# One turn number per piece of work, and the first loads in the order of their first use, in a fused decoder kernel

## The reference

```
out_t = r_t . (u * k_t v_t + s);   s = k_t v_t + w_t * s        (w = exp(-exp(...)))
```

## Time and profile before

| | |
|---|---|
| three runs | 692.63, 693.77, 694.01 us |
| profiled execution | span 694.0 us; no other time is recorded for it |
| busy of the span | TensorE 93%, VectorE 86%, ScalarE 82%, GpSimd 45% |
| mean granted TensorE clock | 0.985 of full |
| moved by DMA | 50.4 MB |

### The profile page before, as it was taken

How to read it: one execution, slowest core, us unless ns; L and a number is a source line. 1 busy time by engine, 2 the same in 40 slices (tenths; PEclk the granted TensorE clock), 3 DMA queues, 4 the chain that set the end, 5 groups by cost and what they waited for, 6 DMA issues and landing times.

```text
span 694.0 us, 17297 instructions
## 1 busy us (share of the span) xinstructions
PE 645.3 (93%) x5877; PEld 561.6 (81%) x5877; DVE 598.2 (86%) x1430; ACT 571.7 (82%) x2071; POOL 311.6 (45%) x440
## 2 busy tenths in 40 slices
PE   6878998999999999999999999999999989898776
PEld 5666787888989888988989888989888877687555
DVE  3598588999999999999999999999999987968274
ACT  1568899899999999999999999999999987664513
POOL 1154252646464554636364646454554624432120
PEclk9999999999999999999999999999999999999799
DMA  8920031221305050504122231305050503120200
GB/s 306 325 70 9 2 104 36 70 70 58 88 9 138 1 146 1 145 2 122 25 85 62 67 81 53 93 4 144 1 146 1 146 0 108 31 70 0 69 9 8
DMA packets 53725, 50.44 MB, mean 73 GB/s; under 512 B 6030, under 2 KB 48902, under 8 KB 53254
## 3 DMA queue, kind: packets, MB, share of 16 engines
q1 hardware_dynamic: 53638, 49.34, 24.7%
HBM read 28.62 MB, written 3.93 MB: 47 GB/s over the span
## 4 chain that ended last, share of the span: by engine, by line
PE 80%; DVE 8%; ACT 7%; issue 3%; POOL 1%; DMA 0%; SPq 0%; DVEq 0%; ACTq 0%; POOLq 0%
PE PS_B L552 16%; PE PS_T L654 9%; PE PS_B L694 8%; PE PS_S L552 7%; PE PS_D L559 5%; PE PS_S L625 4%; PE PS_T L662 4%; PE PS_S L559 4%; PE PS_T L559 4%; ACT SC L1291 3%; PE PS_D L800 2%; PE PS_B L703 2%; PE PS_D L552 2%; ACT PT L1301 2%; PE PS_T L545 2%
## 5 line engine op out<-in xcount | busy, mean ns | idle before, releaser
L1291 ACT ACTIVATE SC<-SC,NMX 128x128 f32<-128x128 f32 x512 | 200.0, 398 | 0.2
L1291 ACT ACTIVATION_READ_ACCUMULATOR SC<-SC,NMX 128x1 f32 x512 | 101.0, 197 | 0.0
L654 PE MATMUL PS_T<-CST,SC 128*128 128x128 f32 x512 | 81.3, 281 | 7.7 <-ACT PT L1301 3.6
L976 DVE TENSOR_REDUCE NMX<-SC 128x4 f32<-128x512 f32 x128 | 85.2, 676 | 0.4 <-POOL SC L1499 0.3
L1301 ACT ACTIVATE PT<-PS_T 128x512 f32<-128x512 f32 x120 | 70.8, 590 | 12.7 <-PE PS_T L654 12.7
L654 PEld LDWEIGHTS PS_T<-CST,SC 128*128 128x128 f32 x512 | 56.4, 141 | 26.1 <-ACT PT L1301 12.7
L1057 DVE TENSOR_TENSOR_SCAN SS<-W,AJ 128x1024 f32<-128x1024 f32 x32 | 73.2, 2288 | 0.2
L552 PE MATMUL PS_B<-MX,W 128*128 128x128 f32 x512 | 64.2, 280 | 4.7 <-ACT KR L1350 4.7
L552 PEld LDWEIGHTS PS_B<-MX,W 128*128 128x128 f32 x512 | 61.3, 196 | 4.9 <-ACT KR L1350 4.9
L1499 POOL TENSOR_TENSOR SC<-SC,MADD 128x512 f32<-128x512 f32 x48 | 59.9, 1276 | 6.5 <-DVE SC L956 6.5
L552 PE MATMUL PS_B<-B_LT,W 128*128 128x128 f32 x512 | 61.1, 278 | 1.0 <-ACT B_LT L1231 0.9
(11 more groups left out here) (231 smaller groups left out, 1595.0 us busy)
## 6 DMA issues: line engine op xcount, KB each, us to landing
W<-EW SPq DMA_DIRECT2D x32, 512.0 KB, 4.1
V<-values_by_head SPq DMA_DIRECT2D x28, 512.0 KB, 5.4
W<-in_weights SPq DMA_DIRECT2D x1, 4160.0 KB, 21.0
ENC<-in_enc SPq DMA_DIRECT2D x16, 128.0 KB, 2.3
out<-X SPq DMA_DIRECT2D x16, 128.0 KB, 5.8
X<-in_x SPq DMA_DIRECT2D x1, 1920.0 KB, 15.7
values_by_head<-VC SPq DMA_DIRECT2D x14, 128.0 KB, 1.8
W<-in_weights SPq DMA_DIRECT2D x1, 1280.0 KB, 8.5
```

The lines of the kernel that those rows point to most:

```text
L654: last = pe.transpose(PS_T[:, j * T:(j + 1) * T], SC[:, nr(b, a) % 2, g, j, :], ident)
L976: dve.tensor_reduce(NMX[:, nr(b, a) % 2, GH * g:GH * g + GH], SC[:, nr(b, a) % 2, g], AX_X, ALU.max, negate=True)\
L1291: last = act.activation(SC[:, nr(b, a) % 2, g, j, :], SC[:, nr(b, a) % 2, g, j, :], ACT.Exp, bias=NMX[:, nr(b, a) % 2, h:h + 1], accum_out ...
```

## The change

Three edits. The pieces and their instances are the same before and after; nothing is computed otherwise.

1. Each entry of an order has a turn number instead of a lag, and a second table, `*_MOVED`, gives single sequences a number of their own. The engine's program is all instances sorted by 10000 b + number, so the order may differ from one sequence to the next. On TensorE 97 of 757 instances that do something leave the old order, on VectorE 273 of 1225, on ScalarE 276 of 897, on GpSimd 64 of 316, on SyncE 25 of 75.
2. The stores of sequences 2 to 11 stand together on SyncE, between `b_vspread@13` and `b_wspread@14`; stores 0 and 1 stand a few sequences later than before.
3. The loads: tokens of sequences 1 and 2 and `enc` of sequence 0 go ahead of the second block of weights, the cross masks of the first three sequences come right behind it, the rest of the tokens and masks behind the third block. A new semaphore `in_next` counts the first three sequences' loads; sequence 3 (`AHEAD`) waits for `in_rest`.

```
-                if 0 <= i - lag < B:
-                    pieces[name](i - lag, arg)
+            for name, arg, b in in_order(order, moved):
+                pieces[name](b, arg)
+def in_order(order, moved):
+    turns = [(TURN * b + moved.get((name, arg), {}).get(b, turn), name, arg, b)
+             for name, arg, turn in order for b in range(B)]
+    return [(name, arg, b) for _, name, arg, b in sorted(turns, key=lambda t: t[0])]
...
             sp.dma_start(MASK[:, B, :], mask_self).then_inc(in_rows, 16)
+            sp.dma_start(X[:, 1:AHEAD, :], x[1:AHEAD].rearrange("b s c -> s b c")).then_inc(in_next, 16)
+            sp.dma_start(ENC[:, :], enc[0]).then_inc(in_enc, 16)
             sp.dma_start(W[:, W_AT["ao"]:W_CUT1], weights[:, W_AT["ao"]:W_CUT1]).then_inc(in_wa, 16)
-            sp.dma_start(ENC[:, :], enc[0]).then_inc(in_enc, 16)
-            sp.dma_start(MASK[:, 0:B, :], mask_cross.rearrange("b q k -> q b k")).then_inc(in_rest, 16)
-            sp.dma_start(X[:, 1:B, :], x[1:B].rearrange("b s c -> s b c")).then_inc(in_rest, 16)
+            sp.dma_start(MASK[:, 0:AHEAD, :], mask_cross[0:AHEAD].rearrange("b q k -> q b k")).then_inc(in_next, 16)
             sp.dma_start(W[:, W_CUT1:W_CUT2], weights[:, W_CUT1:W_CUT2]).then_inc(in_wb, 16)
+            sp.dma_start(X[:, AHEAD:B, :], x[AHEAD:B].rearrange("b s c -> s b c")).then_inc(in_rest, 16)
+            sp.dma_start(MASK[:, AHEAD:B, :], mask_cross[AHEAD:B].rearrange("b q k -> q b k")).then_inc(in_rest, 16)
...
                 elif b == 1:
+                    dve.wait_ge(in_next, IN_REST)
+                elif b == AHEAD:
                     dve.wait_ge(in_rest, IN_REST)
```

More of the change, by code:

```diff
@@ L70 @@
 LAST = 2
+AHEAD = 3
 FIRST = 4
@@ L84 @@
     ('d_keyrec', 0, 15): 4, ('d_val', 0, 15): 2}
+TURN = 10000
 SP_ORDER = [
-    ("b_vspread", 0, 4), ("d_store", 0, 6), ("b_wspread", 0, 3), ("b_vstore", 0, 3), ("a_load", 0, 0)]
-PE_ORDER = [
[L90 to L99, removed]
@@ L100 @@
-DVE_ORDER = [
[L101 to L118, removed]
@@ L133 @@
-POOL_ORDER = [
[L134 to L140, removed]
+    ("a_load", 0, 90000), ("b_wspread", 0, 110006), ("b_vstore", 0, 120002), ("b_vspread", 0, 120004),
@@ new lines @@
+POOL_MOVED = {
+    ("a_root", 0): {0: -50000, 1: -59992, 2: 5517, 3: -623, 6: 487}, ("a_addmask", (0, 0)): {0: -49996, 2: 7940},
+    ("a_addbias", 0): {0: -49990, 1: -59988, 4: 9187, 5: 9655, 6: 9538},
+    ("a_addmask", (0, 2)): {0: -49994, 1: 15130, 2: 8105, 5: 9860, 10: 13909},
+    ("a_root", 1): {1: 18156, 2: 22639, 4: 19843, 9: 22805, 10: 22624, 12: 21685},
+    ("a_addbias", 1): {3: 21198, 4: 19848, 5: 20647, 7: 25047}, ("a_addmask", (1, 0)): {0: 26178, 1: 22179},
+    ("a_addmask", (1, 1)): {0: 27157}, ("a_addmask", (1, 2)): {0: 27334}, ("b_root", 0): {0: 30652, 3: 31569},
+    ("b_addbias", 0): {3: 31704}, ("b_root", 1): {14: 37896}, ("b_shift", 0): {14: 37898},
+    ("b_addnorm", 0): {3: 39134, 12: 39123, 14: 37934},
+    ("b_addnorm", 1): {1: 40305, 2: 39688, 3: 39379, 11: 39691, 12: 39554},
+    ("b_addnorm", 2): {1: 41547, 2: 39851, 3: 41019, 11: 42549, 12: 41745}, ("d_rstate", 0): {13: 47920},
+    ("d_final", 0): {14: 61756},
+}
@@ L409, in tiles, with run @@
             return ap.rearrange("p (t n) -> p t n", t=CT)
-        def run(pieces, order, i):
-            for name, arg, lag in order:
-                if 0 <= i - lag < B:
-                    pieces[name](i - lag, arg)
+        def run(pieces, order, moved):
+            for name, arg, b in in_order(order, moved):
+                pieces[name](b, arg)
         def nr(b, a):
@@ L519, in _ @@
             pieces = named(a_load, b_vstore, b_vspread, b_wspread, d_store)
-            for i in range(B + LAG):
-                run(pieces, SP_ORDER, i)
+            run(pieces, SP_ORDER, SP_MOVED)
             sp.wait_ge(stored, 16 * B)
@@ L864, in _ @@
                            d_own, d_read, d_oturn, d_yturn, d_biasout, d_out, d_turn, d_keyrec, d_val)
-            for i in range(B + LAG):
-                run(pieces, PE_ORDER, i)
+            run(pieces, PE_ORDER, PE_MOVED)
         @block.vector
@@ L952, in a_mask @@
                 if not later(b) and a and g == 0:
+                    dve.wait_ge(in_next, IN_REST)
+                elif b == AHEAD and a and g == 0:
                     dve.wait_ge(in_rest, IN_REST)
@@ L1216, in _ @@
                            d_moments, d_mixed, d_mixing)
-            for i in range(B + LAG):
-                run(pieces, DVE_ORDER, i)
+            run(pieces, DVE_ORDER, DVE_MOVED)
         @block.scalar
@@ L1454, in _ @@
                            b_gatetanh, d_first_states, d_own, d_ocopy, d_squares, d_root_of, d_root, d_affine, d_scale, d_keyrec, d_relu2)
-            for i in range(B + LAG):
-                run(pieces, ACT_ORDER, i)
+            run(pieces, ACT_ORDER, ACT_MOVED)
         @block.gpsimd
@@ L1569, in _ @@
                            d_rstate, d_gates, d_root)
-            for i in range(B + LAG):
-                run(pieces, POOL_ORDER, i)
+            run(pieces, POOL_ORDER, POOL_MOVED)
 def kernel(**inputs):
```

213 lines of the change are left out of this document (200 added, 13 removed), and 3 rows, old and new, of the table PE_MOVED.

## The result

| | before | after |
|---|---|---|
| median of the runs | 693.89 us (692.63 to 694.44, 4 runs) | 682.24 us (680.98 to 683.35, 4 runs) |
| span of the profiled execution | 694.0 us | 681.1 us |

The ratio is 0.9839, with a 95% interval of 0.9817 to 0.986: 11.7 us faster where 13.2 were forecast. Ratios are taken from fast runs only; one run of the kernel before, of 3555 us, counts in none of them. The busy line of the page after answers to the earlier trace rows. The instructions are the same but for two on ScalarE, and TensorE's share rises by one point.

What follows compares the result with a forecast made beforehand. TensorE bounds the middle turns; at the ends it waits on dependent chains. Fill 4.0, middle 0 and drain 9.2 (1.5 + 3.4 + 4.3) sum to 13.2 us off 693.8: 680.6 us, range 675 to 690, chance 0.53.

Steps and rivals of the forecast that it cites:

- the fill: Pipeline start: TensorE's waits for context go (3.0 us) and scores@1 start earlier (1.0); 4.0 us gained, bounds 0 and 8.
- Drain only: Rival: the pipeline's start gains nothing, its chains being as long as before, only its end gains; 684.6 us, chance 0.18.
- the turn grows: Rival: VectorE's new order makes TensorE wait 1.23 us in each of 11 middle turns; 698 us, chance 0.08.
- nothing: Rival: orders differ but every wait is met by another; 693.8 us, chance 0.05.
- the clock stays low: Rival: TensorE's clock stays low at the end, or its moved pieces wait; 686 us, chance 0.16.
- Loads: Start: the tokens' 1.02 us wait goes but ScalarE's exps hide it; counted 0, between -1.0 and +1.0 us.
- The middle: Ten middle turns: d_rstate ahead of b_sum on VectorE just fits the 1.56 us spare; 0, bound 1.2 us a turn.
- (a): First drain step: prob_copy(1,3)@15 goes earlier, decay2@14 behind out@15, W8@14's delay hidden; 0, from -1.5 to +1 us.
- (b): Drain, sequence 15 from low1 to decay1: decay1@15 starts earlier; 1.5 us gained, bounds -1 and 2.5.
- (c): Drain, ScalarE up to KR@15: squares@14 and root moved, two of four table loads go; 3.4 us gained, bounds 2.1 and 3.4.
- (d): Drain, KR@15 to its outer product: yturn@14 between valgate halves, affine@14 ahead of VC; 4.3 us gained, bounds 1.3 and 5.
- Behind the outer product: Last 31.7 us, after sequence 15's outer product: order as before, time unchanged.

Runs made afterwards that it cites:

- experiment 2: New order in the drain only: kernel before, with old loads and old order in the loop's first ten turns, new order behind them; 687.96 us, ratio 0.9914.
- experiment 1: New loads and new order in the fill only (loop's first ten turns), all later pieces ordered as in the kernel before; 688.27 us against 694.09, ratio 0.9915.
- experiments 3 and 4: 3: changed kernel with its loads put back as before, 682.91 us, ratio 0.9844. 4: kernel before with only the new loads, 694.35 us, ratio 1.0007.
- experiment 5: Kernel before with four pieces moved on TensorE alone: scores@1 ahead of out@0, queries of sequences 2 to 4 behind pv; 697.31 us against 694.55, ratio 1.0037.
- experiment 12: Kernel of experiment 1 with VectorE kept in its old order throughout; 706.15 us against 694.39 for the kernel before, ratio 1.0169.
- experiment 8: Changed kernel without the two filler products at a_val@0; 681.97 us, ratio 0.9819 to the kernel before.
- experiment 10: Changed kernel with decay2@14 back ahead of out@15 on TensorE, decay2@14 and decays@14 earlier on ScalarE, so W8@14 comes earlier; 683.07 us, ratio 0.9833.
- experiment 6: Kernel before with five ScalarE pieces moved at the very end (squares, root_of, affine of 14; decays, keyrec of 15); 691.01 us against 694.55, ratio 0.9942.
- experiment 7: Kernel of experiment 6, plus on TensorE yturn@14 between the valgate halves of sequence 15 and out@14 ahead of select@15; 689.14 us, ratio 0.9912.
- eleven fillers: Changed kernel with eleven more filler products at d_keyrec@14, in TensorE's last gap; 679.09 us against 694.12 for the kernel before, ratio 0.9783.

## Why the prediction was right, point by point

**Place.** The gain lies at both ends and none in the middle, as the windows of before said. The total is better than its parts: the fill gave 5.8 us where 4.0 were forecast, and the drain 6.1 (experiment 2, and 6.0 from the fill-only kernel's median to the changed kernel's) where 9.2 were. That 13.2 came so near to 11.7 is in part luck, two errors of opposite sign. "Drain only" (684.6) fell with experiment 1, "the turn grows" (698) with the 372.47 us, "nothing" with the result. Of "the clock stays low" one part is true, at another place: behind the outer product.

**The sum against its own time.** One step was wrong without harm. I put the profiled 694.0 at 0.2 us above the median. A span is not a run's time: the runs record both, and the time is about 1.8 us longer in nearly all of them (682.92 for the span of 681.1). So the profiled execution of before was, by this estimate, one of some 695.8 us, 2 us above the median. Its clock fits this. Two executions of the same orders at that place, the kernel before and the loads-only kernel (windows of TensorE):

```profile
642.00:646.00 4.00, 3.88 (x27) 0.62 0.02 4
562.00:566.00 4.00, 3.31 (x41) 0.64 0.01 2
```

```profile
642.00:646.00 4.00, 3.94 (x40) 1.00 0.02 4
562.00:566.00 4.00, 3.31 (x51) 1.00 0.01 2
```

The gain between the two profiles is 12.9 us, between the medians 11.7.

**Loads: 0.** Right (experiments 3 and 4).

**The fill: 4.0.** Measured 5.8, inside the bounds of 0 and 8. The place of scores@1 was 0.9 us off (31.5 forecast, 32.44), since scores@0 itself was late; from scores@0 to the 11th scores 7.0 us were gained. The first mask of sequence 1 comes 1.1 us earlier (33.60 for 34.67; 1.2 forecast). What failed is the mechanism of the first term: "a query's matmuls take 1.05 us, scores 1.15, more than each wait, so nearly all 3.3 us go". These moves by themselves cost 2.8 us (experiment 5). The gain needs VectorE's order to change with that of the others (experiment 12), and I had priced one engine's waits and not the chain through two. That 4.0 and 5.8 are near each other is luck. Which of VectorE's pieces matter most, and what TensorE's, ScalarE's and GpSimd's orders each add, was not tried. I also overlooked that the first scores may come later: scores@0 starts at 14.65 to 15.96 us in the eight traces with the new order at the start and at 13.78 to 14.85 in the six with the old one, 0.8 us later on the average, and experiment 8 did not find the reason.

**The middle: 0.** Right; `d_rstate` ahead of `b_sum` fits into the 1.56 us.

**(a) 0, from -1.5 to +1.** From the 31st scores to low1@15 the changed kernel is 1.5 us slower in its profile (0.4 + 1.0). Over the traces this stretch varies with the clock, 85.5 to 87.6 us in the seven with the old order there, 87.1 to 88.8 in the five with the new order and no edit to it there; the means are 86.8 and 88.0, some 1.3 us lost by single executions whose ranges overlap. I had looked only at W8@14. It is late as foreseen and costs nothing that can be told (experiment 10). The loss is put down to no piece by a run. TensorE's longest wait there is another one: 2.61 us for B_N before, now 3.08 us for the exps, and the 3.1 us are there in every trace with the new drain order and in none with the old:

```profile
595.11 1.09 PE L832 MATMUL PS_T<-CST,SC 128*128 128x128 f32 x4 [3.08 <-ACT SC L1473]
```

**(b) 1.5.** 2.1 us in the profiles, 1.1 against those executions of the old order that keep the clock there (6.35 or 6.36 us from low1@15 to decay1@15, in five traces). The profile of before overstated it; 1.1 is below the 1.5 forecast and inside the bounds.

**(c) 3.4.** KR@15 comes 3.9 us sooner behind decay1@15 in the profiles, and 3.4 against the loads-only kernel, whose clock is full there (7.75 to 4.32 us): as forecast. ScalarE's part is 2.5 us (from decay1@15 to EW: 5.93 us in the loads-only kernel, 3.45 in experiment 6), and the rest of the drain's order gives 1.0 more (2.49). The row at 643.22 of experiment 6 fits that: squares@14, moved ahead of decay2@15, waits there 1.47 us for VectorE's O and holds up DW, while in the changed kernel TensorE's oturn@14 stands ahead of decay1@15 and this wait is gone. That it is this piece alone was not tried.

**(d) 4.3.** 3.7 us; 3.1 to 3.8 against the five traces with the old order there. "From KR's end ... 5.2" was 5.9: the chain that I followed, through yturn, affine, gated and out@14, came as said (out@14 forecast to end at 4.1, it ended near 4.0), but the outer product also needs `b_select@15`, which now stands behind out@14 on TensorE and takes 1.95 us (the row at 653.10 of experiment 7). VectorE waits 0.78 us for it. I had left this out.

**Behind the outer product: unchanged.** Wrong by 1.1 us, and the order there is not as before: the second half of `b_select@15` no longer stands in the gap ahead of XK. TensorE idles 3.78 us there, not 1.97, and the slow clock of the earlier trace rows is now found behind this wait and not behind KR. Experiment 7, which leaves that half where it was, still idles 1.97 us and takes 13.11 us from the outer product to read@15, the drain-only kernel 14.02. The eleven fillers take the loss back and more (11.87): the kernel before had slow products at that place, too (1.92 us at 669.23 for the four that take 1.03 with the fillers).

**Tables.** Each load is 1.28 us in the rows of before and after, and the next instruction starts right behind it: EARLY at 641.72, with the load from 640.43 to 641.71. The two loads that went were 2.6 us of ScalarE's time. The price of about 2.7 us in the Trainium skill ("ScalarE: Activation LUTs", What ACT_TABLE_LOAD costs) has a drain of its own in it, for which no row here has room.

## What to carry to other kernels

In a pipeline of engines with fixed orders, a wait on one engine does not tell what moving a piece is worth: the same four moves that removed it cost 2.8 us alone and belong to 5.8 us of gain when the consumer's order moves with them. Change the orders of producer and consumer together, and do it at the ends, where the bound engine has idle time; the middle had 1.15 us to give and gave none. Check each part of a sum by a run of its own, since a total can come out near by errors that cancel. Before taking a difference from two profiles, compare executions in which the clock is the same at each landmark, and when a wait has been shortened, look where the clock falls next.

## What the runs showed of the hardware

- The clock falls at some places in one execution and not in another of the same order: 0.64 and 1.00 for 562 to 566 us. The last scores start at 586.88 and 585.37 us in these two, a difference of 1.5 us; by low1@15 it is gone again, since the second execution has its slow stretch later (0.50 for 602 to 606 us, where the first has 0.74). From low1@15 to decay1@15 the two take 7.38 and 6.35 us. Over the runs of the kernel before that are on record, time and mean clock go together: 690.9 to 692.8 us at 0.990 or more, 696.2 to 696.8 at 0.983 or less.
- At the start the same four products took 1.91 and 1.55 us, the same eight 1.67 and 1.05, at a granted clock of 1.00 in both. In the drain the same four-product shape takes 1.91 us, too, where the record says 0.50, so the record of the clock may be wrong at the start; this was not tried.
- 22 filler products of 2.62 us in a gap of 3.94 us kept the clock at 1.00 through the 1.32 us of waiting that was left.
